# Causal attention on one core: VectorE adds the mask of one-head diagonal pieces inside its maximum instruction

## The reference

```python
def _gqa(x, wq, wk, wv, wo):          # 16 heads, 4 key/value heads, head size 16
    ...
    attn = jnp.einsum('bqhd,bkhd->bhqk', q, k) * scale
    causal = jnp.tril(jnp.ones((S, S), dtype=bool))
    attn = jnp.where(causal, attn, jnp.float32(-jnp.inf))
    attn = jax.nn.softmax(attn, axis=-1)
    out = jnp.einsum('bhqk,bkhd->bqhd', attn, v).reshape(B, S, C)
    return out @ wo.T
```

## Time and profile before

| | |
|---|---|
| time, median of 3 runs | 8392.82 us (8388.09 to 8399.02) |
| the profiled execution, its own time | 8391.64 us |
| its span, first to last instruction | 8389.9 us |
| TensorE matmul busy | 7633.5 us (91%) |
| VectorE busy | 7255.9 us (86%) |
| ScalarE busy | 5015.7 us (60%) |
| GpSimd busy | 3693.2 us (44%) |
| maxima (line 833), VectorE | 4608 instructions, 2725.7 us |
| mask matmuls (line 678), TensorE | 4096 instructions, 435.4 us |

### The profile page before, as it was taken

The page is one execution under the profiler, slowest core; times in us unless marked ns, Lnnn a source line. Parts: engine busy times, 40 slices in busy tenths (PEclk is TensorE's granted clock), DMA queues, the critical chain, the costliest instruction groups (busy, mean ns, idle before and its releaser), DMA issues. The chain is left out here.

```text
span 8389.9 us, 132293 instructions
## 1 busy us (share of the span) xinstructions
PE 7633.5 (91%) x40012; PEld 3197.5 (38%) x40012; DVE 7255.9 (86%) x10619; ACT 5015.7 (60%) x7151; POOL 3693.2 (44%) x1326
## 2 busy tenths in 40 slices
PE   6999999989988888888889999898889999999899
PEld 3333333325543333333333333333553333333355
DVE  6988888858877999999999999999658888888588
ACT  3577777773255666566666666666316777777622
POOL 0010000110015999999999999999510001101000
PEclk9899999999999999999999999999988999999999
DMA  6101101112263222222233333333670001010121
GB/s 178 18 19 20 20 19 20 19 33 68 73 205 115 86 84 84 84 84 84 84 95 94 96 95 92 95 93 95 203 223 16 19 20 20 20 27 13 37 80 60
DMA packets 532315, 605.82 MB, mean 72 GB/s; under 512 B 195520, under 2 KB 344768, under 8 KB 527616
## 3 DMA queue, kind: packets, MB, share of 16 engines
q1 hardware_dynamic: 527104, 564.73, 22.8%
q0 software_dynamic: 4608, 33.56, 2.0%
HBM read 399.85 MB, written 163.69 MB: 67 GB/s over the span
## 5 line engine op out<-in xcount | busy, mean ns | idle before, releaser
L833 DVE TENSOR_REDUCE ffn_att_mx<-psum 128x1 f32<-128x512 f32 (+3 forms) x4608 | 2725.7, 652 | 357.2 <-PE psum L674 204.1
L794 ACT ACTIVATE ffn_att_e<-psum,unscale 128x1024 f32<-128x1024 f32 (+3 forms) x2560 | 2376.8, 985 | 756.5 <-PE psum L739 750.5
L1695 POOL TENSOR_TENSOR scan_h<-scan_h,scan_cs 128x2048 f32<-128x2048 f32 x512 | 2334.8, 4626 | 228.1 <-ACT scan_state L1871 228.1
L1779 PE MATMUL psum<-scan_h,ident 128*128 128x512 f32 x4096 | 1961.5, 624 | 108.1 <-POOL scan_h L1695 108.0
L1998 DVE TENSOR_TENSOR_SCAN scan_h<-psum,scan_state,scan_db 128x512 f32<-128x512 f32 x1408 | 1677.4, 1261 | 10.6 <-ACT psum L1911 10.6
L641 POOL TENSOR_SCALAR_AFFINE_SELECT ffn_att_e<-ffn_att_e 128x512 f32<-128x512 f32 x512 | 324.6, 634 | 3012.3 <-ACT ffn_att_e L794 3012.3
L674 PE MATMUL psum<-ffn_att_k,ffn_att_q 48*128 48x512 f16 (+3 forms) x5120 | 1435.6, 367 | 174.7 <-DMA ffn_att_v<-v 59.2
L705 PE MATMUL psum<-ffn_att_e,ffn_att_v 128*32 128x512 f32 (+3 forms) x10240 | 1238.1, 556 | 8.1 <-ACT ffn_att_o L809 2.6
L1779 PEld LDWEIGHTS psum<-scan_h,ident 128*128 128x128 f32 x4096 | 795.6, 199 | 1176.6 <-issue 1038.5
L1911 ACT ACTIVATE psum<-scan_dt,scan_anr 128x512 f32<-128x512 f32 x1024 | 700.0, 686 | 542.5 <-DVE scan_h L1998 542.2
L1911 ACT ACTIVATE psum<-scan_dt,scan_anf 128x512 f32<-128x512 f32 x1024 | 699.8, 686 | 534.5 <-DVE scan_h L1998 533.9
(11 more groups left out here) (252 smaller groups left out, 7319.9 us busy)
## 6 DMA issues: line engine op xcount, KB each, us to landing
scan_cs<-scan_bcd SPq DMA_DIRECT2D x520, 256.0 KB, 3.1
scan_bs<-scan_bcd SPq DMA_DIRECT2D x162, 256.0 KB, 3.4
scan_win<-xp SPq DMA_DIRECT2D x34, 1036.0 KB, 7.0
scan_dt<-scan_sp POOLq DMA_DIRECT2D x32, 1024.0 KB, 6.9
mamba_out_ffn_in_ys<-both SPq DMA_DIRECT2D x18, 1024.0 KB, 7.7
mamba_out_ffn_in_zt<-zs SPq DMA_DIRECT2D x18, 1024.0 KB, 10.6
scan_yi<-y SPq DMA_DIRECT2D x17, 1024.0 KB, 6.7
ffn_att_q<-q_parts SPq DMA_DIRECT2D x128, 128.0 KB, 2.9
```

The source lines that it names most:

```text
L794: nc.scalar.activation(E[:, s % PB, 2 * hp:2 * hp + 2, off:CH], psum[:, 2 * hp:2 * hp + 2, off:CH], ACT.Exp, scale=unscale[:, 0:1]).then_i ...
L833: nc.vector.reduce_max(mx[:, hh * 2 + pairs[0]:hh * 2 + pairs[1], i // HALF, i % HALF, c // TT], psum[:, turn, 0:(pairs[1] - pairs[0]) * w ...
L1695: nc.gpsimd.tensor_tensor(h[n % NH][:, :, :], h[n % NH][:, :, :], cs[:, n % NCS, :].unsqueeze(1).to_broadcast([P, DM, CH]), ALU.mult).then ...
L1779: ins = nc.tensor.matmul(psum[:, m, :], ident[:, :], h[n % NH][:, m, :], start=False, stop=n == DS - 1)
```

## The change

The mask of a diagonal piece of one head is no longer added by TensorE. `edge` is a new tile of 128 x 512 f32: zeros, with the causal triangle of -3e38 in its last 128 columns. For these pieces (list `alone`, 32 in a round) VectorE executes `tensor_tensor_reduce` instead of `reduce_max`. It adds the last w columns of `edge` to the scores, multiplies by 1.0, writes the sum back to PSUM, and gives the maximum in its accumulator output. Diagonal pieces of two heads and all other pieces stay as they were.

```diff
+    alone = [n for n, (i, c, _, pairs, _) in enumerate(pieces) if c + TT > i and pairs[1] - pairs[0] == 1]
...
+        edge = sb("edge", [P, CH])
...
-        N_MADE = 3 * NBUF + 2
+        N_MADE = 3 * NBUF + 3
...
-                sp.wait_ge(made, N_MADE + 2)
+                sp.wait_ge(made, N_MADE + 3)
...
+                nc.gpsimd.affine_select(out=edge[:, CH - P:CH], in_=edge[:, CH - P:CH], compare_op=ALU.is_ge, fill=NEG, base=0,
+                                        pattern=[[-1, P]], channel_multiplier=1).then_inc(made, 1)
...
-                    is_diag = c + TT > i
+                    is_diag = c + TT > i and n not in alone
...
+                nc.vector.memset(edge[:, :], 0.0).then_inc(made, 1)
...
                 def reduce(it, n, turn):
                     i, c, w, pairs, hh = pieces[n]
-                    dve.wait_ge(m_ps, it * NP + n + 1)
                     if n == 0 and not (isinstance(it, int) and it == 0):
                         dve.wait_ge(n_max, 2 * it - 1)
                     if n == NP0:
                         dve.wait_ge(n_max, 2 * it)
+                    if n in alone:
+                        hold(dve, m_ps, it * NP + n + 1, dve_passed)
+                        score = psum[:, turn, 0:w]
+                        nc.vector.tensor_tensor_reduce(score, score, edge[:, CH - w:CH], 1.0, NEG, ALU.add, ALU.max,
+                                                       mx[:, hh * 2 + pairs[0], i // HALF, i % HALF, c // TT:c // TT + 1]).then_inc(m_red, 1)
+                        return
+                    dve.wait_ge(m_ps, it * NP + n + 1)
...
                 dve.wait_ge(recip, 1)
+                dve.wait_ge(made, N_MADE + 3)
```

More of the change, by code:

```diff
@@ L545, in attention @@
         m_high, m_low, m_in = sem("m_high"), sem("m_low"), sem("m_in")
-        sp_passed, pool_passed, pe_passed = sem("sp_passed"), sem("pool_passed"), sem("pe_passed")
+        sp_passed, pool_passed, pe_passed, dve_passed = sem("sp_passed"), sem("pool_passed"), sem("pe_passed"), sem("dve_passed")
         s_ps, e_ready, masked, pv = sem("s_ps"), sem("e_ready"), sem("masked"), sem("pv")
@@ L647, in _ @@
                 pe.sem_inc(pv, PV0)
-                pe.wait_ge(made, N_MADE + 2)
+                pe.wait_ge(made, N_MADE + 3)
                 def bank_is_free(when, it, use):
```

## The result

The changed kernel takes 8423.05 us (median; 8412.89 to 8431.42) against 8389.05 us before (8379.02 to 8410.95) in the same sessions: the ratio is 1.0036, 95% interval 1.0028 to 1.0044. It is slower, as forecast and inside the range, but by 34 us, not by the 97 us of the sum. The profiled execution's span is 8425.9 us, 36 us more than before's 8389.9.

A forecast was written before the change was run, and what follows sets the result against it. VectorE was taken to bound most of a round. Added work +133, gaps -38 and set-up +2 gave +97 us on the profiled 8391.64: 8488.7, stated as 8490 us to allow for the median; 8-in-10 range 8368 to 8630.

The forecast's parts named there:

- the sum: Whole kernel: added VectorE work +133, gaps won back -38, set-up +2, together +97 us.
- the price of 0.13 us a piece: VectorE's 1,024 new instructions: about 0.065 us for the read-out plus 0.065 us of lost overlap each, 133 us in all.
- one of the three signs of being wrong: Profile after: read-out takes no slot of its own, round shrinks although VectorE's work grew, or duration far from 0.68 us.
- my lower end: VectorE's accumulator read-out: 0.0 us if it goes on wholly under the next instruction.
- The streaming rate: New VectorE instruction: neither the second source nor the second operation costs anything; rate that of the maxima, 0.61 us start to start.
- The rival of half rate: New VectorE instruction: running maximum makes each column wait for the last, 573 us more, 8889 us in all; chance 0.08.
- TensorE waits for it, but ... it is not the late one: PSUM bank released at the read-out, 0.13 us later; no cost, because VectorE is behind by as much.
- `hold` costed at nothing: Separate wait and semaphore increment ahead of each new VectorE instruction: free; at the gaps some tens of nanoseconds, five places a round.
- The gaps, -38 us,: Five places a round where VectorE idles behind mask matmuls: 1.2 us a round won back, ends 19 and 79 us.
- the filling, 0.5 us: Before the gaps of 0.80 and 0.64 us: four longer one-head VectorE instructions ahead of them fill 0.5 us.
- The set-up, +2 us,: Start of each of two attention phases: one memset and one GpSimd select ahead of first loads, about 1 us each.
- the rival "even": Whole kernel: extra price 0.04 to 0.07 us a piece with 57 to 60 us back, 8376 to 8410 us; chance 0.12.

The follow-up runs named there:

- The two ceiling kernels: Kernel before without TensorE's masks for one-head diagonal pieces, nothing in their place: 0.9935; the same plus a separate wait and increment ahead of these maxima: 0.9968.
- the two halves: Each against the kernel before: VectorE adds the masks while TensorE keeps its own, 8446.23 us; TensorE's one-head masks left out with nothing in their place, 8333.40 us.
- steps 9 to 11 alone: Change only for query tiles 2 and 3, sums written to SBUF, sixteen small memsets added per attention phase, against the kernel before: 8384.94 us, 0.9996.

## Why the prediction was wrong

The forecast was slower, and slower it is, but by a third of the size, and the direction came out in part by luck, as the last paragraphs say. By its own steps:

- **What it adds, the price of 0.13 us a piece: this is the term that failed.** It was made of a slot of 0.065 us for the read-out and 0.065 us because "the next maximum can no longer start under the last one's tail". Neither is there. The read-out lies under the next instruction, which starts where the last one's streaming ends. What is left is 0.03 us from start to start, from the write to PSUM: 1,024 x 0.03 = 31 us, and by busy time 47.4 us (0.046 a piece), against 133. That the read-out takes no slot of its own is one of the three signs of being wrong that the prediction names. ScalarE's read-out, which I read as not overlapping at all, in fact starts 0.10 us before its ACTIVATE ends (1966.24 against 1965.92 + 0.42); it was no guide to VectorE's, and my lower end, "wholly under the next instruction", was the truth about the slot. The Trainium skill, page "VectorE: DVE Perf Modes", section "Two Vector instructions with no wait between them", which I cited for the two instructions, also has the rule on this: a Vector instruction is held until the earlier ones have finished if its input starts in another group of 32 partitions than the last one read from that memory, or its output in another than the last one written to it. The tiles of these instructions all start at partition 0, so by this rule nothing is held back, and the timeline agrees.
- **The streaming rate** was right: with the sum in SBUF the two durations are 687 and 553 ns against 682 and 548. The rival of half rate is out.
- **"TensorE waits for it, but ... it is not the late one"**, of the bank's later release, stands at the two places that looked like its price: the matmul starts 0.86 us after the first of the three in kernels that release the bank 0.68 and 0.79 us after an instruction's start.
- **`hold` costed at nothing** failed: 0.68 us in a round. At a piece whose scores are there it is free, as I had said, and some cost "at the gaps" I had foreseen too, but put at "some tens of nanoseconds"; it is 0.11 us at six places and 0.03 at a seventh. The two ceiling kernels are 0.0033 apart, 28 us, which is nearly the whole of the loss.
- **The gaps, -38 us,** were not right in their parts. The masks alone are worth 1.5 us in a round and not 0.6, because they are on the path at ten places and not at five; the filling, 0.5 us, is not seen as a term of its own. In the changed kernel VectorE idles 0.8 to 1.2 us less in a round at full clock, 27 to 39 us.
- **The set-up, +2 us,** was right: from VectorE's first write to the tile of v to the phase's first score matmul for the maxima it is 1.1 us more in each phase. The memset took 0.48 us and the select 0.29.
- **The clock** was not in the sum at all. In the profiled pair there are 46 us more at half clock in the rounds, at the 0.32 to 0.41 us that such a us costs (a round of 98.2 with 12.0 us takes some 102.0; one of 97.6 with 3.4 us takes 99.0): 15 to 19 us. On the mean of all timed executions the kernels differ by 28 us (standard error 7), which is 6 to 12 us of time at 0.22 to 0.41.

By place the sum of the profiled pair is +2 (set-up) + 1.4 (the pieces ahead of round 0) + 2.2 (the first rounds) + 29.8 (the 30 rounds, of which 14 are the growth of a round at full clock and the rest goes with the clock) = +35 us, against 36 measured. The growth of single rounds at full clock is: masks away -1.5, `hold` +0.7, the new instruction +0.75, its write to PSUM +0.5, together +0.45 us. These are differences of medians of few rounds, before's of four.

Two kinds of error worked against one another: the instruction was far cheaper than its price and the masks dearer, and costs put at zero (the separate wait, the clock) took what this would have won. With a price of 0.03 and nothing else, the sum would have been 8393 + 2 + 31 - 38 = 8388: the rival "even", and also wrong. So that the time lies in the range, and that the kernel is slower at all, is not to the credit of the price that the forecast rested on.

Open stays what sets the length of a half-clock stretch, and with it why the two halves do not add up: the same matmuls gave 717, 747, 794 and 799 us in the whole kernel, by the means, with different work on VectorE. The time at half clock is long where the masks are gone and the new instruction stands in steps 3, 4 and 9 to 11, and not with either half alone, nor with steps 9 to 11 alone (764); no run shows why. Also not tried: the new instruction with no separate wait, since the kernel writes its wait that way, so `hold` was measured only on the plain maximum.

## What to carry to other kernels

When work is moved from one busy engine to the other, run the two halves alone: the one without the replacement is the ceiling, and here it was 0.65% for the masks. Half of it went to a wait written as an instruction of its own. But the halves need not add up: here the other half, measured alone, cost 55 us, and the two together 34 us instead of nothing, with the difference in TensorE's clock. So measure the combination as well, and look at the granted clock of all executions before reading a clock effect out of one. Merged rows hide short gaps, and the idle time in front of a weight load is not that of the matmul: follow one piece from engine to engine before naming what it waits for. Price an accumulating instruction by its start-to-start distance, not by the sum of the two rows that it leaves, and send an output that nobody reads to SBUF. When an untouched phase changes its time, look for waits on "issue" and for packets on the instruction queue before giving the edit the blame or the credit.

## What the runs showed of the hardware that was not expected

- VectorE's accumulator read-out takes 141 ns if the main instruction writes PSUM and about 80 ns if it writes SBUF, and in both cases it lies under the next instruction, unless that one reads the result: the negated maximum starts 0.82 us after the last new instruction with the sum in PSUM, 0.73 with it in SBUF, 0.71 after a plain maximum. The read-out's own row (1,024 of them, 144.4 us) therefore overstates its price.
- Writing 512 columns to PSUM instead of SBUF cost 718 - 687 = 31 ns, 384 columns 587 - 553 = 34 ns: about the same for both widths.
- A wait with an increment of its own ahead of a VectorE instruction delayed it by 0.11 us where VectorE stood waiting for TensorE (0.15 instead of 0.04 us behind the matmul's end) and by 0.01 us at most where the scores were there already: 0.68 us in a round with 32 of them.
- With TensorE busy for more than 90% of a round, its granted clock fell to 0.50 (1.2 GHz) in stretches of 3.4 to 13.7 us, in the same steps of many rounds. A us at half clock cost about a third of a us in such a round. Taking the same masks off TensorE lowered the time at half clock by 53 us in one kernel and raised it by 39 in another, where VectorE's instruction was the new one.
- Where a loop's code lies in VectorE's stream moved an untouched phase by 39 us (469 against 430), with six waits of up to 8.0 us and 35 packets instead of 6 on the instruction queue.
